# One transfer instead of two for the high and the low part of each K and Q tile

## The reference

```
xn = layernorm(x)
q, k, v = xn @ Wq.T, ctx @ Wk.T, ctx @ Wv.T          # 16 heads of 32
p = exp(clip(q k^T / sqrt(32), -50, 50)); attn = p / sum(p)   # the mask is all ones
x = x + (attn @ v) @ Wo.T
l = layernorm(x); sl, sr = absmax(l by row)/127, absmax(rhs by column)/127
x = x + (round(l/sl) as int8) @ (round(rhs/sr) as int8) * sl * sr
```

## Time and profile before

| What | us |
|---|---|
| Median of 3 runs | 1823.92 |
| Lowest, highest run | 1823.84, 1828.95 |
| The profiled execution | 1825.44 |
| Its span | 1823.6 |
| TensorE busy in it | 1745.1 (96%) |
| VectorE, ScalarE, GpSimd busy | 1365.7, 1308.8, 318.0 |
| Mean granted clock of TensorE | 0.986 of full speed |

### The profile page before, as it was taken

The page is one execution under the profiler, slowest core; times in us unless marked ns, Lnnn a source line. Parts: engine busy times, 40 slices in busy tenths (PEclk is TensorE's granted clock), DMA queues, the critical chain, the costliest instruction groups (busy, mean ns, idle before and its releaser), DMA issues.

```text
span 1823.6 us, 30572 instructions
## 1 busy us (share of the span) xinstructions
PE 1745.1 (96%) x10872; PEld 1005.2 (55%) x10872; DVE 1365.7 (75%) x1554; ACT 1308.8 (72%) x1715; POOL 318.0 (17%) x169
## 2 busy tenths in 40 slices
PE   6999999999999999999999999999998999999976
PEld 5995555555555565656655565656664333333333
DVE  4657777777778878788876878888785777777746
ACT  4557777778777777777777777877776777777733
POOL 0000111101112112120211212121120212212122
PEclk9999999999999999999999999999999999999987
DMA  6686565556655665667565566746654464647242
GB/s 243 212 237 164 139 155 140 141 141 156 157 141 145 176 163 144 171 165 200 122 151 153 138 185 160 197 118 173 164 133 136 105 146 98 157 94 163 58 132 88
DMA packets 224703, 276.31 MB, mean 152 GB/s; under 512 B 27168, under 2 KB 141856, under 8 KB 224032
## 3 DMA queue, kind: packets, MB, share of 16 engines
q1 hardware_dynamic: 222816, 271.14, 56.9%
q10 hardware_dynamic: 1728, 3.15, 0.7%
HBM read 181.41 MB, written 92.54 MB: 150 GB/s over the span
## 4 chain that ended last, share of the span: by engine, by line
PE 79%; DVE 6%; issue 6%; DMA 3%; ACT 3%; POOL 2%; SPq 1%; POOLq 0%; DVEq 0%; ACTq 0%
PE scores L824 24%; PE tile L802 23%; PE wsum L840 21%; DVE acc L1291 4%; PE scores L802 3%; PE tile L867 3%; ACT probs L1015 2%; PE tile L861 1%; DMA q_parts<-stage_hi 1%; PE tile L928 1%; DMA k_parts<-q_stack 1%; POOL rstd L1353 1%; PE tile L905 1%; POOL sums L1342 1%; DMA probs<-x 0%
## 5 line engine op out<-in xcount | busy, mean ns | idle before, releaser
L1015 ACT ACTIVATE probs<-scores 128x1024 f32<-128x1024 f32 x1024 | 993.8, 1026 | 248.9 <-PE scores L824 243.6
L1291 DVE TENSOR_TENSOR acc<-acc,probs 128x2048 f32<-128x2048 f32 x376 | 905.4, 2408 | 113.2 <-ACT probs L1015 95.0
L824 PE MATMUL scores<-q_stack,k_stack 128*128 128x512 f32 x2048 | 611.2, 417 | 29.6 <-ACT probs L1015 29.0
L824 PEld LDWEIGHTS scores<-q_stack,k_stack 128*128 128x128 f32 x2048 | 346.2, 188 | 381.6 <-ACT probs L1015 238.3
L840 PE MATMUL wsum<-probs,v_sb 128*32 128x512 f32 x4096 | 506.6, 601 | 0.0
L1353 POOL TENSOR_TENSOR rstd<-var_eps,minus_half 128x1 f32<-128x1 f32 x56 | 96.3, 1719 | 829.3 <-DVE var_eps L1190 829.3
L840 PEld LDWEIGHTS wsum<-probs,v_sb 128*32 128x32 f32 x4096 | 103.6, 109 | 237.7 <-issue 218.7
L1242 DVE TENSOR_TENSOR squares<-squares 128x128 bf16<-128x128 bf16 x160 | 35.4, 221 | 123.1 <-ACT squares L1055 122.7
L802 PE MATMUL tile<-ctx_hi,wk_hi 128*128 128x256 f32 x412 | 115.4, 280 | 1.8 <-DVE ctx_lo L1200 1.8
L802 PE MATMUL tile<-ctx_hi,wk_lo 128*128 128x256 f32 x412 | 115.1, 279 | 0.0
L802 PE MATMUL tile<-ctx_lo,wk_hi 128*128 128x256 f32 x412 | 115.1, 279 | 0.0
(11 more groups left out here) (196 smaller groups left out, 1898.7 us busy)
## 6 DMA issues: line engine op xcount, KB each, us to landing
k_stack<-k_parts SPq DMA_DIRECT2D x248, 256.0 KB, 7.0
q_stack<-q_parts SPq DMA_DIRECT2D x124, 256.0 KB, 6.8
v_parts<-v_stage SPq DMA_DIRECT2D x64, 256.0 KB, 6.9
v_sb<-v_parts SPq DMA_DIRECT2D x64, 256.0 KB, 7.1
raw<-ctxT SPq DMA_DIRECT2D x27, 512.0 KB, 6.3
k_parts<-stage_hi SPq DMA_DIRECT2D x96, 128.0 KB, 3.2
k_parts<-stage_lo SPq DMA_DIRECT2D x96, 128.0 KB, 2.0
k_parts<-q_stack SPq DMA_DIRECT2D x64, 128.0 KB, 4.6
```

Of the source, the lines that this page charges most:

```text
L824: last = nc.tensor.matmul(scores[:, h, :], k_stack[:, kt // 4, h, (kt % 4) * P:(kt % 4 + 1) * P], q_stack[:, qb, h, :], start=True, stop=True)
L1015: nc.scalar.activation(probs[:, slot % RING, 2 * pair:2 * pair + 2, :], scores[:, 2 * pair:2 * pair + 2, :], ACT.Exp, scale=1.0 / math.sqr ...
L1291: nc.vector.tensor_tensor(acc[:, :, :], other, probs[:, slot % RING, :, :], ALU.add).then_inc(sems["add_done"], 1)
```

## The change

The two staging buffers become one array with an axis for the part, and the two stores of a tile become one of 256 KB whose source and destination both run over partition, part and column. SyncE waits for the high part, then for the low part, then issues it. Where there were eight semaphores for landed stores (`hi_stored0` to `3`, `lo_stored0` to `3`) there are four, `parts_stored0` to `3`. ScalarE's copy of a high part and VectorE's subtraction for a low part now wait for the same one.

```diff
     **{f"{part}_stored{n}": (lambda seg, n=n: 0 if not seg.a else 16 * STAGED // 4 if not seg.b else 16 * STAGED // 2 if n < 2 else 0)
-       for part in ("hi", "lo") for n in range(4)},
+       for part in ("parts",) for n in range(4)},
...
-        stage_hi = sb("stage_hi", [P, 2, ROWS], F32R)
-        stage_lo = sb("stage_lo", [P, 2, ROWS], F32R)
+        stage = sb("stage", [P, 2, 2, ROWS], F32R)
+        stage_hi, stage_lo = stage[:, 0], stage[:, 1]
...
+        def parts_of(seg, n):
+
+            return stage[:, :, n, :] if seg.b else stages_alone[:, :, n, :]
...
             def all_parts_stored(ct, *others):
-                for n in [f"{part}_stored{n}" for part in ("hi", "lo") for n in range(4)] + list(others):
+                for n in [f"parts_stored{n}" for n in range(4)] + list(others):
                     ct.wait_alone(sp, n, 0)
...
-                            for part, ready, src, stored in ((0, "hi_done", hi, f"hi_stored{n}"), (1, "lo_done", lo, f"lo_stored{n}")):
-                                ct.wait_alone(sp, ready, seen_hi)
-                                sp.dma_start(dst[(b + 1) * G + m, part, :, at:at + width], src.bitcast(F32)).then_inc(sems[stored], 16)
+                            ct.wait_alone(sp, "hi_done", seen_hi)
+                            ct.wait_alone(sp, "lo_done", seen_hi)
+                            sp.dma_start(dst[(b + 1) * G + m, :, :, at:at + width].rearrange("a p t -> p a t"), parts_of(seg, n).bitcast(F32)) \
+                                .then_inc(sems[f"parts_stored{n}"], 16)
...
-                        ct.wait(act, f"hi_stored{n}", 16 * before)
+                        ct.wait(act, f"parts_stored{n}", 16 * before)
...
                             for n in range(4):
-                                for part in ("hi", "lo"):
-                                    ct.wait(act, f"{part}_stored{n}", 0)
+                                ct.wait(act, f"parts_stored{n}", 0)
...
-                        ct.wait(dve, f"lo_stored{n}", 16 * before)
+                        ct.wait(dve, f"parts_stored{n}", 16 * before)
```

## The result

| | median | lowest to highest | runs |
|---|---|---|---|
| before | 1825.23 us | 1821.53 to 1830.16 | 20 |
| changed kernel | 1831.71 us | 1826.92 to 1837.75 | 20 |

The changed kernel is slower by a third of a per cent: the ratio is 1.0034, with a 95% interval of 1.0025 to 1.0044. The prediction was 1825.9 us, with a range up to 1829.5. Of the miss, 1.3 us come from the base, since the median of 20 runs of the kernel before is that much above the three that the prediction started from; 4.5 us come from the change itself, +6.5 us where +2.0 was worked out (the means of the 20 runs differ by 1832.02 - 1825.47 = 6.6 us, and by 5.3 us against 1826.76 us, the mean of the 71 runs of the kernel before that stand beside the experiments). The profiled execution of the changed kernel took 1834.49 us, span 1832.7 us.

A forecast was written before the change was run, and what follows sets the result against it. TensorE bounds the kernel, so transfers cost time only where it waits. The terms 0.28 + 1.72 + 0 + 0 + 0 gave +2.00 us on 1823.92, making 1825.9 us, range 1822.1 to 1829.5.

The forecast's parts named there:

- C: Rival, faster: fewer, larger transfers shorten the queue at the three stalls, giving back 9.3 us, to 1814.6 us; chance 0.05.
- B: Rival, slower: the two-piece store lands far later at the three stalls, clock adding; 1835 us (+5.5 or more), chance 0.09.
- the signs that were named: Chain steps of 6.5 to 7.7 us, ScalarE's store waits some 18 us, TensorE's exponential waits about 31 us.
- Item 1: Kernel start, fifth tile's copy: the pair lands at 26.33 us against 26.05 for the high part, +0.28 us.
- Item 2: Q tiles around 520, 945 and 1372 us: copy waits for the low part's landing too, 0.26, 1.26, 0.20, together 1.72 us.
- Item 3: Same three places: first Q tile's high part, stored later, directly ahead of the `k_stack` loads; 0, upper end 1.1 us.
- Item 4: All other ScalarE copies: stores landed or nearly, 2.6 us of cover at the tightest; cost 0, upper end 1.5 us.
- Issue: SyncE's queue: 192 issues of 0.3 to 0.5 us go, none on the chain; 0, at best a 1.8 us gain.
- item 5: VectorE's subtraction waits for the same semaphore, but behind ScalarE's copy, which has waited already; cost 0.
- size: Merged 256 KB store: lands in 2.0 to 2.3 us on an idle queue, 0.2 to 0.5 above the small one; no cost.

The follow-up runs named there:

- U and L: Kernel before, two transfers a tile and eight semaphores kept, both issued only once the low part is there, ScalarE's copy waiting for both; ratio 1.0031, 1832.19 us.
- U: Kernel before, two transfers issued where they were, only ScalarE's copy of a high part waits for both of them; ratio 1.0013, 1829.01 us.
- L: Kernel before, two transfers a tile issued only when the low part is there, ScalarE's copy waiting for the high one alone; ratio 1.0008, 1827.75 us.

## Why the prediction was wrong

- **The mechanism and the places** were right. The bound was the same, the same three stalls grew, ScalarE's large waits for stores stayed at three places, and no rival took over: no gain of the queue (C), and the merged form is not slow in itself (B's reason; U and L are as slow without it). What was wrong is the size, in two terms put at nothing and one cost left out of the sum. Of the signs that were named, the steps of 6.5 to 7.7 us came out at 6.86, 8.52 and 8.05, ScalarE's waits at 19.8 us instead of 18, and TensorE's at 33.4 instead of 31.
- **Item 1, the start:** +0.28 us predicted, -0.15 us seen (the copy at 25.97 instead of 26.12). The whole stretch to the fifth segment is the same, 142.6 and 142.5 us.
- **Item 2, the landing:** 1.72 us for three places, read from the low stores' own landings. U, which adds exactly this wait, made the kernel slower by 0.13% (0.02 to 0.24%), 2.4 us. At the three places it added 1.4 us ahead of the copies. The rule "the low store's recorded landing is the merged store's" held as far as it went.
- **Item 3, the high part held back:** this is the first step that failed. I put it at 0, "the 128 KB fit into a hole", with 1.1 us as the upper end. The landings grew by 3.14 us, 1.42 us more than item 2: above even that end. L alone, which only holds the high part back, adds 1.7 us ahead of the copies, and both together 4.4. The hole at 518 us was real, but the DMA engines are full before that store has landed (1.03 and 1.16 of their time at 526 and 527 us). That the bytes put in front of the queue therefore come out at its end is my reading; the runs show the delay, not its path. In runs, adding L to U takes the ratio from 1.0013 to 1.0031, 3.2 us by the medians, partly here (places 102.8 to 105.1 us) and partly elsewhere (between, 1159.6 to 1162.1).
- **The clock, left out of the sum.** I named it in rival B alone. It belongs in each sum that lengthens or shifts a stall. Of the 5.0 us that the places grew, 3.1 are landing, 0.5 the later issue, and 1.4 lie behind ScalarE's copy, where the half-clock stretch is twice as long in the changed trace (3.4 instead of 1.7 us of missing clock at each place). The length is in part the luck of these two traces: the kernel merged everywhere but there has the long one at all three places with almost the stalls of before, and pays 2.6 us behind the copies for it; L has the short one with longer stalls and pays nothing. But it isn't all luck. The mean granted clock of the whole kernel is 0.9825 over the 20 runs of the change and 0.9849 over 71 runs of the kernel before (standard errors 0.0004 and 0.0001), which makes an estimated 0.0024 x 1832 = 4.4 us more of missing clock; U has 0.9838, U and L 0.9836, L 0.9849. Not all of that is time, since some of it falls where TensorE stands still.
- **Item 4, everywhere else:** the second step that failed. I took the tightest place, found 2.6 us of cover and called the rest free. The runs with the stalls away show 2 to 6 us, and the profiles some 2 of them between the places. My upper end of 1.5 us was for "a handful of places"; there are 180 tiles. In the changed trace the copy of the earlier trace rows was idle for 0.90 instead of 0.73 us, about the 0.2 us that I expected, and the exponentials behind it still ended before TensorE needed them (243.59 against 246.00 us), so the loss is not at the place I looked at. I had asked only for the copies that wait for the stores I changed; the likely place, not tested, is a copy that waits for another store in the same queue, V's.
- **Issue, item 5, size:** nothing speaks against the zeros. K's stores land in 2.2 us in the median, inside the 2.0 to 2.3 that I gave.

- **A slip in rival B:** 3 x 1.8 is 5.4 and not above 5.5 us; with the start's 0.28 it passes. Nothing hangs on it.

The sum as the traces have it: 3.1 for the landings, 0.5 for the later issue, 1.4 for the clock behind them, about 2 between them, some 7 us, against 6.5 by the medians and 5.3 to 6.6 by the means. It is read from the traces that it explains, so it is an account and no second prediction. What stays open is the part of the 4.0 us (2 to 6) without stalls that "between" does not cover, whether V's buffer is all of the rest, and whether the four semaphores cost something in the tail.

## What to carry to other kernels

A merged transfer is not priced by the transfer: it starts with its later half and frees the buffer with its later half, and where a queue of loads stands between, both delays add up at its end (1.4 and 1.7 us apart, 4.4 together), so a hole in front of a full stretch is no cover. Before merging a small store, look at what is queued ahead of it: here moving 1 MB of loads behind one store was worth 19 us by the means (1826.8 and 1807.8 us), three times what the merge cost. And where a kernel is bound by one engine, a cost too small to show in any one wait can still add up over 180 tiles (here some 2 us between the places); more runs, and not a closer look at one trace, bound it.

## What the hardware did that I had not expected

**A stall of TensorE is followed by a half-clock stretch of one of two lengths.** Windows of the kernel with U, around the same first place:

```profile
528.00:529.00 1.00, 0.00 (x0) 0.00 (x0) 0.31 (x2) 0.97 (x3) 0.00 (x0) 0.55 0.14 47
...
534.00:535.00 1.00, 1.00 (x4) 0.72 (x3) 1.00 (x1) 0.00 (x0) 0.00 (x0) 0.53 0.12 45
535.00:536.00 1.00, 1.00 (x8) 0.48 (x10) 1.00 (x1) 0.63 (x1) 0.00 (x0) 1.00 1.04 383
```

and of the kernel with L:

```profile
529.00:530.00 1.00, 0.49 (x2) 0.30 (x2) 0.56 (x2) 1.00 (x2) 0.00 (x0) 1.00 0.06 20
530.00:531.00 1.00, 0.82 (x3) 0.50 (x2) 0.60 (x1) 1.00 (x3) 0.05 (x1) 0.62 0.40 133
...
533.00:534.00 1.00, 1.00 (x4) 0.77 (x4) 1.00 (x1) 0.00 (x0) 0.82 (x1) 0.68 0.00 0
```

With a share x of a microsecond at 0.50, the mean is 1 - x/2. So in U the clock fell at about 528.1 us, with TensorE still idle, and was back at 534.9; in L it fell at 530.2, when TensorE had begun again, and was back at 533.6. ScalarE's wait at this place was nearly the same in both, 5.8 and 5.9 us. The stretch lasts 6.8 us in the one and 3.4 in the other, which is the 3.4 and 1.7 us of missing clock.

Which one follows goes with the moment of the fall, in all 21 stalls of the seven traces that have them. In the 14 long cases the clock fell 0.4 to 3.1 us before TensorE began again; in the 7 short ones it fell between 0.4 us before that and 1.4 us after it. What sets that moment these runs do not isolate. In the kernels with the moved loads, without a stall, there is no such stretch at these places; near the end of every trace, in the last 60 us, there are longer ones, of 10 us and more.

**VectorE's normalisation takes nearly three times as long when it begins together with GpSimd's product.** In the tail the same instruction, 128x512 fp32 with two scalars for each partition, comes eight times, 136 times in the 17 traces. It took 1.49 to 1.59 us in the 41 cases where it began from 0.03 us before to 0.07 us after the start of GpSimd's product, and 0.54 to 0.55 us in the other 95, where it began at least 0.16 us ahead of the product or met none. The changed kernel, then the one before with the moved loads (the first repeat; start us, us, engine, instruction):

```profile
1604.40 1.28 POOL L1336 TENSOR_TENSOR sums<-sums,denoms 128x512 f32<-128x512 f32 x1
1604.47 1.50 DVE L1228 TENSOR_SCALAR normed<-xr,mean_var,rstd 128x512 f32<-128x512 f32 x1 [0.44 <-POOL rstd L1357]
...
1609.23 0.73 PE L829 MATMUL scores<-q_stack,k_stack 128*128 128x512 f32 x2 [1.95 <-ACT probs L1020]
```
```profile
1577.82 0.55 DVE L1227 TENSOR_SCALAR normed<-xr,mean_var,rstd 128x512 f32<-128x512 f32 x1 [0.44 <-POOL rstd L1356]
1578.14 1.38 POOL L1335 TENSOR_TENSOR sums<-sums,denoms 128x512 f32<-128x512 f32 x1 [0.35 <-DMA denoms<-recip_row]
...
1581.63 0.73 PE L827 MATMUL scores<-q_stack,k_stack 128*128 128x512 f32 x2 [0.98 <-ACT probs L1018]
```

TensorE then waits 1.95 instead of 0.98 us for the exponential behind it. In the case of 0.55 us GpSimd waited 0.35 us for a load of reciprocals (256 KB) and so began later; which case comes flips from one trace to the next. It goes with the tail: four of the eight take 1.5 us or so in the traces with tails of 422.9 to 424.9 us, one in those with 415.8 to 416.4 us and in one with 420.3. In the five traces with four semaphores it is 3.6 of the eight on average, in the other twelve 1.9. The Trainium skill ("GPSIMD Engine Reference", section "Specifications") has GpSimd share its SBUF interfaces with VectorE, in contention with VectorE instructions that have two SBUF inputs or run in a two-port mode. Contention agrees with the trace, 1.50 against 0.55 us; this instruction has one tensor input and scalars, and whether it runs in such a mode no run here shows.
